# An attention and FFN kernel in float32 pieces: P is moved in place under two names, and three heads of the last batch are moved too

## The reference, cut to what matters

```python
def _L0_attn_ref(x, w_qkv, b_qkv, w_o, b_o):      # x: 8 x 512 x 1024, 8 heads of 64
    qkv = x @ w_qkv.T + b_qkv
    q, k, v = jnp.split(qkv, 3, axis=-1)           # then to_heads: b, h, s, 64
    scores = jnp.einsum('bhfc,bhtc->bhft', k, q)
    causal = jnp.triu(jnp.ones((s, s), dtype=bool))
    scores = jnp.where(causal[None, None], scores, MASKED_BIAS)
    attn = jax.nn.softmax(scores, axis=-2)
    vals = jnp.einsum('bhft,bhfc->bhtc', attn, v)
    return vals.transpose(0, 2, 1, 3).reshape(b, s, PART) @ w_o.T + b_o

x = x + _layernorm(_L0_attn_ref(_layernorm(x), ...))
x = x + _layernorm(_L0_ffn_ref(_layernorm(x), ...))   # x @ W.T + b and a routed low-rank part
```

## Time and profile before

| | us |
|---|---|
| median of 3 runs | 1414.14 |
| lowest, highest | 1413.69, 1414.88 |
| the profiled execution | 1414.13 |
| its span, first to last instruction | 1412.3 |
| TensorE busy | 1396.6 (99%) |
| VectorE busy | 1046.3 (74%) |
| GpSimd busy | 704.1 (50%) |
| ScalarE busy | 692.8 (49%) |
| DMA queue q1, of 16 engines' span | 35.3% |

### The profile page before, as it was taken

The page is one execution under the profiler, slowest core; times in us unless marked ns, Lnnn a source line. Parts: engine busy times, 40 slices in busy tenths (PEclk is TensorE's granted clock), DMA queues, the critical chain, the costliest instruction groups (busy, mean ns, idle before and its releaser), DMA issues.

```text
span 1412.3 us, 25002 instructions
## 1 busy us (share of the span) xinstructions
PE 1396.6 (99%) x7796; PEld 1247.1 (88%) x7796; DVE 1046.3 (74%) x2204; ACT 692.8 (49%) x1498; POOL 704.1 (50%) x1268
## 2 busy tenths in 40 slices
PE   7999999999999999999999999999999999999998
PEld 6888888888888888888888889999999999999997
DVE  7676685776775776766756888898878787878764
ACT  6365465564573664654654764433333333333332
POOL 3364462571562553644624775555555555555542
PEclk9999999999999999999999999999999999999999
DMA  7434334324433343343333643322222222222311
GB/s 253 142 127 120 143 104 154 134 95 138 145 111 123 126 137 138 115 127 138 112 99 94 213 139 116 104 107 98 96 92 101 104 104 91 90 94 96 119 75 60
DMA packets 71797, 168.55 MB, mean 119 GB/s; under 512 B 7760, under 2 KB 31568, under 8 KB 71760
## 3 DMA queue, kind: packets, MB, share of 16 engines
q1 hardware_dynamic: 71760, 168.09, 35.3%
HBM read 62.15 MB, written 25.69 MB: 62 GB/s over the span
## 4 chain that ended last, share of the span: by engine, by line
PE 91%; issue 3%; POOL 2%; DVE 1%; POOLq 1%; ACT 1%; DMA 1%; DVEq 1%; SPq 0%; ACTq 0%
PE ps_f L2471 23%; PE ps_o L1503 21%; PE ps_o L1534 12%; PE ps_s L1554 6%; PE ps_o L2356 6%; PE ps_v L1370 6%; PE ps_t L1408 3%; PE ps_o L1497 3%; PE ps_z L2356 2%; PE ps_f L2417 2%; PE ps_o L1573 2%; PE ps_x L2407 1%; PE ps_v L1378 1%; PE ps_t L1503 1%; PE ps_o L1454 1%
## 5 line engine op out<-in xcount | busy, mean ns | idle before, releaser
L2471 PE MATMUL ps_f<-wagh,x2Th 128*128 128x364 f32 x756 | 250.9, 332 | 0.0
L2471 PE MATMUL ps_f<-wagh,x2Tl 128*128 128x364 f32 x756 | 248.7, 329 | 0.0
L2471 PE MATMUL ps_f<-wagl,x2Th 128*128 128x364 f32 x756 | 248.3, 329 | 0.0
L1503 PE MATMUL ps_o<-xTh,wh 128*128 128x512 f32 x424 | 172.3, 406 | 0.0
L1503 PE MATMUL ps_o<-xTh,wl 128*128 128x512 f32 x424 | 166.5, 393 | 0.0
L1503 PE MATMUL ps_o<-xTl,wh 128*128 128x512 f32 x424 | 165.7, 391 | 0.0
L583 POOL TENSOR_SCALAR pr<-pr,nwm,rden 128x512 f32<-128x512 f32 (+3 forms) x256 | 159.7, 638 | 11.3 <-issue 11.3
L559 POOL TENSOR_TENSOR cw<-wm,cnt 128x4 f32<-128x4 f32 x64 | 12.8, 200 | 300.3 <-ACT pr L1134 300.3
L2471 PEld LDWEIGHTS ps_f<-wagh,x2Th 128*128 128x128 f32 x756 | 142.0, 188 | 2.2 <-issue 0.3
L2471 PEld LDWEIGHTS ps_f<-wagl,x2Th 128*128 128x128 f32 x756 | 142.3, 188 | 1.5
L2471 PEld LDWEIGHTS ps_f<-wagh,x2Tl 128*128 128x128 f32 x756 | 142.3, 188 | 0.0
(11 more groups left out here) (309 smaller groups left out, 3438.3 us busy)
## 6 DMA issues: line engine op xcount, KB each, us to landing
p_words<-pr SPq DMA_DIRECT2D x56, 448.0 KB, 2.8
kst<-kst SPq DMA_DIRECT2D x64, 256.0 KB, 3.7
x<-in_x SPq DMA_DIRECT2D x31, 512.0 KB, 3.9
x2r<-x2n SPq DMA_DIRECT2D x30, 512.0 KB, 2.9
xs<-in_x SPq DMA_DIRECT2D x24, 512.0 KB, 4.6
out<-x SPq DMA_DIRECT2D x23, 512.0 KB, 2.7
p_words<-pr SPq DMA_DIRECT2D x56, 192.0 KB, 2.3
xs_words<-xs SPq DMA_DIRECT2D x21, 512.0 KB, 3.2
```

Source lines behind the costliest of these rows:

```text
L1503: done = pe.matmul(ps[:, :], w[:, k, c:c + P], xT[:, k, :], start=(k == 0 and w is wh and xT is xTh), stop=(k == KD - 1 and w is wl), skip ...
L2471: last = pe.matmul(ps_f[:, g, 0:GW], a[:, k, :], w[:, k, cols], start=(k == 0 and a is xh and w is wagh), stop=False, skip_group_check=True)
```

## The change

`pr` and `p_words` are now allocated at one address (`pr` in a block that is left again before `p_words` is allocated), so that each move reads and writes the same bytes and only gives them their other type. `ones` goes ahead of both, and all smaller tensors behind them lie 10 KB lower in each partition. In the last batch, `MOVED_LAST` names heads 1, 2 and 4: `sync` moves their P by `move_p`, and `transpose_p` waits for `p_moved` and transposes words, where it waited for `p_ready` and transposed float32. Heads 0, 3, 5, 6 and 7 of the last batch stay as they were. The argument `moved` of `transpose_p` becomes `last_batch`; the calls in the loop now pass `False`, with the effect that they had before.

```diff
--- before.py
+++ after.py
@@ -172,6 +172,8 @@
         ([("q", 3, 0, SECOND)], []),
     ]
 
+    MOVED_LAST = (1, 2, 4)
+
     TURNED = {2: [(0, 0), None, (0, 1)], 3: [(1, 0), (1, 1), (2, 0)], 4: [(2, 1), (3, 0), (3, 1)]}
     X_SLOT = 5
     BARE = 6
@@ -213,9 +215,10 @@
         v = sb("v", [P, NT, NH, 2 * HD], F32R)
         PT = sb("PT", [P, ROOM * P], F32R)
         totals = sb("totals", [P, NH, 2 * HD], F32R)
+        ones = sb("ones", [P, 2], F32R)
+        with ExitStack() as early:
+            pr = sb("pr", [P, 2, PT_N], F32, early)
         p_words = sb("p_words", [P, 2, PT_N], F32R)
-        ones = sb("ones", [P, 2], F32R)
-        pr = sb("pr", [P, 2, PT_N], F32)
         maskf = sb("maskf", [P, P], F32)
         masked = sb("masked", [P, 1], F32)
         cnt = sb("cnt", [P, 4], F32)
@@ -468,8 +471,10 @@
                     load_next(n)
                 for n in range(2):
                     load_vals(n)
+                move_p(1, b)
                 store_vals(0, b)
                 dup_k(2, b)
+                move_p(2, b)
                 store_vals(1, b)
                 sp.wait_ge(W.v_ready, 1)
                 load_vals(2)
@@ -485,6 +490,7 @@
                 sp.dma_start(W.gb_s, gb.partition_broadcast(P)).then_inc(W.gb_landed, 16)
                 for n in W.wag[3:5]:
                     load_next(n)
+                move_p(4, b)
                 store_vals(2, b)
                 sp.wait_ge(W.v_ready, 2)
                 load_vals(3)
@@ -1387,11 +1393,16 @@
                                  start=(part is VSUM_HIGH), stop=(part is VSUM_LOW))
             last.then_inc(totals_full, 1)
 
-        def transpose_p(pe, h, g, b, moved=False):
+        def transpose_p(pe, h, g, b, last_batch=True):
             H = 8 * b + h
+            moved = not last_batch or h in MOVED_LAST
             if g == 0:
+                if last_batch:
+                    moves = 4 * b + sum(m % 2 == h % 2 and m <= h for m in MOVED_LAST)
+                else:
+                    moves = 4 * b + h // 2 + 1
                 if moved:
-                    pe.wait_ge(p_moved[h % 2], 32 * (4 * b + h // 2 + 1))
+                    pe.wait_ge(p_moved[h % 2], 32 * moves)
                 else:
                     pe.wait_ge(p_ready, H + 1)
                 if h > 0:
@@ -1610,7 +1621,7 @@
                         scores(h, b)
                     if h == NH + 1:
                         half_step(h, 0, 0, b)
-                        transpose_p(pe, NH - 1, 2, b, True)
+                        transpose_p(pe, NH - 1, 2, b, False)
                         half_step(h, 0, 1, b)
                     else:
                         steps(h, 0, b)
...
```

More of the change, by code:

```diff
@@ L1624, in body @@
                     if 1 <= h <= NH and h not in (1, BARE, NH):
-                        transpose_p(pe, h - 1, 0, b, True)
-                        transpose_p(pe, h - 1, 1, b, True)
+                        transpose_p(pe, h - 1, 0, b, False)
+                        transpose_p(pe, h - 1, 1, b, False)
                     if h == 2:
@@ L1642, in body @@
                     if 1 <= h < NH:
-                        transpose_p(pe, h - 1, 2, b, True)
+                        transpose_p(pe, h - 1, 2, b, False)
             def last_body(b):
```

## The result

| | before | after |
|---|---|---|
| median of 6 runs, us | 1414.43 | 1426.54 |
| lowest, highest | 1413.69, 1415.59 | 1425.55, 1428.01 |
| the profiled execution | 1414.13 | 1425.55 |
| its span | 1412.3 | 1423.7 |
| mean granted clock | 0.999 | 0.996 |

The account below looks back on a forecast made before the run. The prediction took TensorE, busy 99% of the span, to bound the kernel. Its terms, -0.6 + 4.4 + 6.25 - 0.5 + 2.1 = +11.6 us on 1414.13, gave 1425.7 us, range 1418.5 to 1430.5.

Parts of the forecast that it names:

- The bound: Whole kernel: TensorE is busy 99% of the span, so shorter instructions and waits there both count at full length.
- The transposes: Last batch, three moved heads: transposing words instead of float32 saves 0.2 us a head, 0.6 us in all.
- Head 1's move: Last batch: the move lands late behind wo_raw and vraw loads, so TensorE waits 4.4 us (2.5 to 5.8).
- Head 2's move: Last batch: nothing large is issued ahead, the move lands in time, no wait, 1.8 us to spare.
- Head 4's move: Last batch: the move lands late behind the FFN weight burst; TensorE waits 6.25 us (4.35 to 7.65).
- What else is queued behind: Last batch, after the moves: no other transfer becomes the next wait; TensorE's small later gaps shrink, giving back 0.5 us.
- In place: Loop: moving P onto its own bytes costs 0, with 0.5 us either way for seven rounds.
- The clock: Last batch: the granted clock falls to 0.50 once, in head 4's wait, and costs 2.1 us.
- number 1: Last batch: both waits but no fall of the clock, or a short one; +9.6 us, 1423.7; chance 0.3.
- number 2: Last batch: only head 4 waits, head 1's moves pass the vraw packets; +5 to +8 us; chance 0.06.
- number 3: Last batch: SBUF-to-SBUF transfers pass those waiting for HBM, so no waits; -0.6 us, 1413.5; chance 0.08.
- number 4: Loop: the move in place is slower than between buffers, adding 6.3 us in seven rounds; 1432.0; chance 0.06.

Follow-up runs that it names:

- e2: The changed kernel with only head 1 of the last batch moved: 1419.05 us, ratio 1.0036 to the kernel before.
- e5: The changed kernel with head 1's move issued ahead of the four wo_raw and two vraw loads, head 4's as it is: 1419.29 us, ratio 1.0038 to before.
- e3: The changed kernel with only head 2 of the last batch moved: 1412.50 us, ratio 0.9989 to the kernel before.
- e4: The changed kernel with only head 4 of the last batch moved: 1420.05 us, ratio 1.0040 to the kernel before.
- e12: The changed kernel with only head 4 moved, its two DMAs issued ahead of the last two FFN weight chunks: 1417.98 us, ratio 1.0026 to before.
- e7: The changed kernel with only head 4 moved, its two DMAs issued by ScalarE on its own queue: 1421.28 us, ratio 1.0055 to before.
- e1: The changed kernel with no head of the last batch moved, in place in the loop only: 1412.80 us, ratio 0.9993 to the kernel before.
- e11: The changed kernel with no last-batch head moved, P in place, 10 KB left empty so small tensors keep old places: 1413.26 us, ratio 0.9994 to before.

## Why the prediction was right

The forecast of +11.6 us met +12.1 in the medians and +11.4 in the profiled executions. By its steps:

- **The bound.** Right. The waits went into the time at their full length.
- **The transposes.** 0.2 us a head forecast; head 2's eight took 0.64 us to the next product and 0.30 us to the one after, against 0.79 and 0.31. TensorE's lag on the kernel before shrinks by 0.15 us there. Seen in the trace, too small for the medians.
- **Head 1's move.** 4.4 us forecast, 4.41 measured. That the figures agree so closely is luck: the wait was 4.85 us in e2, and in the change its parts were 2.8 us for what stands ahead and 1.6 for the move's own bytes, where 2.5 and 1.9 were forecast. That the order alone makes this wait is shown by e5.
- **Head 2's move.** No wait, as forecast (e3). Its first part took 4.6 us to land, not under 3, but the last was there at 778.4, long before TensorE wanted it at 782.50.
- **Head 4's move.** 6.25 us forecast, 5.08 measured, within the bounds set for bytes that cost nothing or all. The difference lies mostly in what stands ahead: 3.5 us, 4.35 forecast; its own bytes took 1.6 again. With head 4 alone it was 7.16 (e4). The step rests on how fast a burst of loads drains, taken from one execution; that is where its uncertainty lies, more than in the move's own bytes. Those took 1.6 us both times, nearer to the 1.5 that the prediction worked out and set aside than to its 1.9.
- **What else is queued behind.** Nothing became the next wait, as forecast. The 0.5 us given back from TensorE's small gaps did not all come: behind head 5's transposes 0.15 us did, behind those at 836.07 the next product came after 1.03 us, 1.15 before, and by the end of the span nothing of that is left.
- **In place.** No wait in the loop was added. The gain of 0.1 us a round was not foreseen; 0 with 0.5 us either way was the term, 0.8 us came.
- **The clock.** The mechanism was right, and so was the price of the fall that it counted: 2.1 us forecast, 2.08 measured behind head 4's wait, some 2.2 without the shorter transposes in it. The step "it fell 4.9 us after the last product; head 4's wait is longer than that, head 1's shorter, so I expect one fall" is the one that failed. It fell behind both waits, and the fall behind head 1's cost another 1.45 us, 3.5 in all where 2.1 stood. A wait of 4.41 us was enough, in e12 one of 2.66.
- The errors had opposite signs: the waits 0.9 us too long (with the restart behind them), the clock with the transposes 1.9 too cheap, the gaps 0.3 too generous, and the 1.7 us that the start and the loop gave were in no term. That the total came out closer than its parts is luck.

The rivals: number 1 (no fall) is refuted by the windows and number 2 (one wait only) by the timeline; number 3, transfers within SBUF going ahead of those that wait for HBM, by the landings of 7 to 8.5 us and again by e7; number 4 by e1 and e11.

## What to carry to other kernels

Before a transfer is put on a path that the busiest engine waits for, look at what lands around its issue, not at how long the data have been ready or how busy the queue is on average: in the trace of before P had been ready for 8.8 us at head 1 and 3.1 us at head 4, and the queue was used 35% of the span, but both moves came behind a burst. Another queue did not help, another place in the order did. Reckon a wait of the busiest engine at more than its length where TensorE is concerned, since the slower clock behind it can add to it, here 3.5 us to waits of 9.5.

## What the runs showed of the hardware that I had not expected

- The time from TensorE's last product to the fall of the clock is no constant. At the kernel's end in the trace of before it was 4.9 us; behind head 1's values 5.1 us (761.7 to the first low window at 766.8), at head 4 3.2 to 3.3 us (801.1 to 804.4), with head 4 alone (e4) some 2 us (796.0 to the window of 798). At head 1 TensorE was working again for 0.7 us when it fell. In e12, with a wait of 2.66 us, the clock fell when TensorE was working again, too. One case of it, as I had it, supports no threshold.
- A second DMA queue with 0.66 MB beside one with 4.99 MB had no packet for 4.6 us after the issue and then took about half of the engines' time; its moves landed after 8.1 and 9.1 us, against 8.3 to 10.3 in the shared queue (e7; the change, e4, e5).
- A copy onto its own source lands like one between two buffers: medians of the two parts 2.7 and 2.2 us in place, 2.8 and 2.3 before.
- With `ones` ahead of `p_words`, which then begins 8 bytes later, the loop's rounds are 98.50 to 98.56 us, in place or not, and 98.64 to 98.67 without. Why is open.
